# Storing one row block of every eighth tile group in four pieces, so that the 16 DMA engines carry unequal shares

## The chip, the cores and the metric

The kernel runs on one core of a Trainium2 chip. The metric is the device time of one execution in microseconds (us); lower is better. Before the change it is 1296.68 us, the median of three runs (1296.31 to 1297.33).

## What is computed

The input `x` is 8 x 32 images of 512 x 512 in float32. Every group of two channels is normalized (mean and variance over both images), the result goes through three levels of a wavelet pyramid, and `x` is added:

```python
def _wavelet_pyramid(x, levels=3):
    K = outer([.25,.5,.25], [.25,.5,.25])
    result = x
    for level in range(levels):
        sh, sw = (H // 2 ** level, W // 2 ** level)
        approx = conv2d(result[:, :, :sh, :sw], K, padding='SAME')
        result[:, :, :sh // 2, :sw // 2] = approx[:, :, ::2, ::2]
    return result
x = x + _wavelet_pyramid(group_norm(x, G=16))
```

Each level replaces the top left quarter of the region before by its smoothed and halved picture. Everything outside the top left 256 x 256 of an image is only `x + normalized x`. So 268.4 MB are read, 268.4 MB are written, and each element is scaled at least once.

## The kernel before

The 256 images make 128 groups of two channels. A group is one tile of 128 partitions x 4096 float32, 2 MB (16 KB per partition): partition p holds, for each of the two channels and each half of the image, two adjacent image rows. So the tile has four row blocks of 4 KB per partition (channel 0 top half, channel 0 bottom half, channel 1 top half, channel 1 bottom half), and in the DRAM a block of one partition is 4 KB on end. `xs` has eight such tiles, the slots; group n lies in slot n mod 8 and stays there from its load to its store, being changed in place. Sixteen laps of eight groups make the 128 groups.

- **SP** only issues the loads (L149), one DMA of 2 MB per group, in order. From the second lap on each first waits until the store of the group that had the slot before has landed (L148).
- **VectorE** (DVE), once a load has landed, makes horizontal sums of column pairs and of row pairs (L322, L328, L334), then adds the pyramid's results into the tiles of the two groups before (L294, L297, and L309 for the corner of the third level).
- **TensorE** does the vertical part of the three levels as matmuls, and the sums over partitions for mean and variance.
- **ScalarE** (ACT) makes the moments (L452, L457), the square root (L477), moves results out of PSUM (L468, L469, L484) and scales each tile by 1 + r (L491, L496). **GpSimd** (POOL) makes the small coefficients and the pair sums.

In step u of a lap the vector engine begins group u, its level 1 is added one step later (`LAG`), and its corner two steps later (`LAG_L3`). ScalarE also issues the stores: in `step` it calls `store(lap, u - LAG_L3)` right after the moments of group u. `store` (L499) waits on three semaphores and then issues one DMA of 2 MB (L505). The DMA issue stands in ScalarE's own instruction stream, so what follows on that engine (L491 first) isn't dispatched before it. The last two groups are stored in halves of 1 MB by `store_half` (L508, L515) at the end. A DMA adds 16 to its semaphore when it has landed in full.

Each of these DMAs is laid out as 128 partitions x 4 blocks of 4 KB: 512 packets, which over 16 engines are 32 packets and 128 KB for each engine.

Of the kernel before, what the change touches and what calls it, by code (L numbers as in the profile page):

```python
# [10 lines left out]
P = 128  # L11
HP = P // 2
EPS = 1e-5
CG = 2
HALVES = 2
RPP = 2
SLOTS = 8
LAG = 1
LAG_L3 = 2
PAD = 2  # L20
# [2 lines left out]
def pyramid_kernel(nc: bass.Bass, x: bass.AP, out: bass.AP):  # L23
    B, C, H, W = x.shape
# [4 lines left out]
    W1, W2, W3 = W // 2, W // 4, W // 8  # L29
    assert H == HALVES * RPP * P and G % SLOTS == 0 and G > SLOTS and CG * W1 <= 512  # L30

    def groups(a):
        return a.rearrange("b (g c) (f p s) w -> (b g) p (c f) (s w)", c=CG, f=HALVES, s=RPP)

    x_dram = groups(x).rearrange("(l k) p h n -> l k p h n", k=SLOTS)
    out_dram = groups(out).rearrange("(l k) p h n -> l k p h n", k=SLOTS)
    out_half = groups(out).rearrange("(l k) p (c f) n -> l k f p c n", k=SLOTS, f=HALVES)

    with ExitStack() as ctx:  # L40
        def sb(name, shape, dt=F32):
            return ctx.enter_context(nc.sbuf_tensor(name, shape, dt))
# [4 lines left out]
        def sem(name):  # L47
            return ctx.enter_context(nc.semaphore(name))

        xs = sb("xs", [P, SLOTS, ROWS * W])
        h1 = sb("h1", [P, 2, ROWS, W1])
# [36 lines left out]

        x_loaded = [sem(f"x_loaded{i}") for i in range(SLOTS)]  # L90
        x_stored = [sem(f"x_stored{i}") for i in range(SLOTS)]
# [28 lines left out]
        LAPS = G // SLOTS  # L120
# [3 lines left out]
        def exists(base, k):  # L124
            return not isinstance(base, int) or 0 <= base + k < G

        def later(base, k, n):
            return not isinstance(base, int) or base + k >= n

        def rows(slot):  # L130
            return xs[:, slot, :].rearrange("p (r w) -> p r w", w=W)

# [8 lines left out]
        def whole(slot):  # L141
            return xs[:, slot, :].rearrange("p (h n) -> p h n", n=RPP * W)

        @block.sync
        def _(sp):
            def load(lap, slot):
                if later(lap, 0, 1):
                    sp.wait_ge(x_stored[slot], 16 * lap)  # L148
                sp.dma_start(whole(slot), x_dram[lap, slot]).then_inc(x_loaded[slot], 16)  # L149

            for lap in range(LAPS):
                for slot in range(SLOTS):
                    load(lap, slot)

            for slot in range(SLOTS):
                sp.wait_ge(x_stored[slot], 16 * (LAPS + (slot >= SLOTS - LAG_L3)))

        @block.gpsimd
        def _(pool):  # L160
# [83 lines left out]
            def step(lap, u):  # L244
                base = lap * SLOTS
                k = u - LAG
                if exists(base, k):
# [29 lines left out]
        def _(dve):  # L277
# [34 lines left out]
            def step(lap, u):  # L312
                base = lap * SLOTS
                b = u % 2
                k = u - LAG
                make = exists(base, u)
# [35 lines left out]
        def _(pe):  # L352
# [69 lines left out]
            def step(lap, u):  # L422
# [5 lines left out]
                if exists(base, u):  # L428
                    level1(base, u)
                if exists(base, u - LAG):  # L430
                    level2(base, u - LAG)

# [10 lines left out]
        def _(act):  # L443
# [55 lines left out]
            def store(lap, k):  # L499
                n = lap * SLOTS + k  # L500
                slot, back = k % SLOTS, k // SLOTS
                act.wait_ge(scaled, n + 1)
                act.wait_ge(l1_added, n + 1)
                act.wait_ge(l2_added, n + 1)
                nc.scalar.dma_start(out_dram[lap + back, slot], whole(slot)).then_inc(x_stored[slot], 16)  # L505

            def store_half(lap, k, f):  # L508
# [8 lines left out]
            def step(lap, u):  # L517
                base = lap * SLOTS
                make, done = exists(base, u), exists(base, u - LAG)
                if make:  # L520
# [3 lines left out]
                if done:  # L524
                    scale_beside(base, u - LAG)
                if make:
# [32 lines left out]
```

## Time and profile before

| what | value |
|---|---|
| median of three runs | 1296.68 us |
| the profiled execution | 1297.06 us |
| its span, first to last instruction | 1295.1 us |
| DVE / ACT / PE / POOL busy | 93% / 88% / 86% / 58% of the span |
| DMA traffic | 537.03 MB in 135213 packets, mean 415 GB/s |
| granted TensorE clock, mean | 0.991 |

The span and the profiled time differ by 2.0 us, which lie around the instructions. Busy shares are means over the whole run; where a stretch of the run matters, the views were asked for that stretch alone. "DMA share" is the mean busy share of the core's 16 DMA engines; packets overlap a little, so that a full house reads as 1.02 or 1.03. The records name the queue of a packet (q1 holds the loads issued by SP, q10 the stores issued by ACT) but not its engine.

### The profile page before, as it was taken

What the parts mean: (1) busy time and instruction counts of PE and PEld (TensorE: products, weight loads), DVE (VectorE), ACT (ScalarE), POOL (GpSimd) and SP (SyncE); (2) the same over time, 40 slices, a digit from 0 to 9 for tenths busy, and PEclk for the clock granted to TensorE, in tenths of its full rate; (3) what the DMA queues carried; (4) which work ended last, traced back from release to release, by engine and by line L of the source; (5) the groups of instructions that cost most, each with busy time, mean ns of one, the idle gap of its engine ahead of it and who ended that gap; (6) DMA issues with size and microseconds to landing.
All of it is one profiled execution on the core that took longest, in us unless ns stands there. A gap on an engine that the chain in (4) does not pass through costs nothing.

```text
span 1295.1 us, 18208 instructions
## 1 busy us (share of the span) xinstructions
PE 1114.5 (86%) x5120; PEld 608.6 (47%) x5120; DVE 1201.6 (93%) x1536; ACT 1139.1 (88%) x1282; POOL 754.1 (58%) x1445
## 2 busy tenths in 40 slices
PE   5888888888888888888888888888898888888884
PEld 2544444444444444444444444444444444444443
DVE  5899999999999999999999999999899999988994
ACT  4999999999999999999999999999898988879985
POOL 3565665665665666566566566566455654554652
PEclk9999999999999999999999999999999999999998
DMA  9999999999999999999999999999999999999996
GB/s 376 409 419 420 420 421 421 421 421 421 421 422 421 421 421 422 421 421 421 421 421 421 421 421 421 421 421 421 421 421 421 421 421 421 420 414 414 418 407 255
DMA packets 135213, 537.03 MB, mean 415 GB/s; under 512 B 4128, under 2 KB 4128, under 8 KB 135200
## 3 DMA queue, kind: packets, MB, share of 16 engines
q1 hardware_dynamic: 67584, 268.44, 50.7%
q10 hardware_dynamic: 67616, 268.44, 50.5%
q8 instruction: 5, 0.08, 0.0%
q14 instruction: 8, 0.07, 0.0%
HBM read 268.44 MB, written 268.44 MB: 415 GB/s over the span
## 4 chain that ended last, share of the span: by engine, by line
DVE 44%; issue 20%; PE 16%; DMA 13%; ACT 5%; ACTq 1%; DVEq 0%
DVE h L328 16%; DVE xs L297 12%; DMA y_dram<-xs 8%; DVE h L322 7%; DVE xs L294 6%; DMA xs<-x_dram 4%; PE mean_ps L365 3%; PE l_ps L416 3%; PE l_ps L419 2%; PE l_ps L417 2%; PE l_ps L418 2%; ACT squares L457 2%; ACT xs L496 1%; DVE ve L284 1%; DVE r L283 1%
## 5 line engine op out<-in xcount | busy, mean ns | idle before, releaser
L266 POOL TENSOR_TENSOR l_pad<-l_pad,col_fix 128x4 f32<-128x4 f32 x128 | 241.7, 1888 | 484.7 <-ACT l_pad L469 484.7
L457 ACT ACTIVATE squares<-xs,negm 128x4096 bf16<-128x4096 f32 x128 | 474.8, 3709 | 4.2
L322 DVE SCALAR_TENSOR_TENSOR h<-xs 128x2048 f32<-128x2048 f32 x128 | 293.6, 2294 | 14.5 <-DMA xs<-x_dram 10.8
L328 DVE SCALAR_TENSOR_TENSOR h<-xs,h 128x2040 f32<-128x2040 f32 x128 | 291.1, 2274 | 0.0
L496 ACT ACTIVATE xs<-xs,negmr,r_plus 128x2048 f32<-128x2048 f32 x128 | 267.9, 2093 | 0.0
L297 DVE SCALAR_TENSOR_TENSOR xs<-l_pad,r,xs 64x256 f32<-64x256 f32 x256 | 205.2, 841 | 1.8
L491 ACT ACTIVATE xs<-xs,negmr,r_plus 128x1024 f32<-128x1024 f32 x128 | 157.4, 1230 | 27.3 <-issue 27.3
L365 PE MATMUL mean_ps<-hsum,mean_w 128*128 128x1 f32 x256 | 49.1, 261 | 144.3 <-DVE h L328 144.3
L309 DVE SCALAR_TENSOR_TENSOR xs<-l_ps,r,xs 64x256 f32<-64x256 f32 x256 | 123.0, 480 | 46.9 <-PE l_ps L419 45.0
L334 DVE SCALAR_TENSOR_TENSOR a<-h 128x1024 f32<-128x1024 f32 x128 | 158.1, 1235 | 4.4
L223 POOL TENSOR_TENSOR newt<-r,half_t 128x1 f32<-128x1 f32 x128 | 148.5, 1160 | 0.0
L379 PE MATMUL l_ps<-h,w_even 128*64 128x512 f32 x256 | 139.9, 629 | 0.0
L380 PE MATMUL l_ps<-h,w_prev 128*64 128x512 f32 x256 | 139.9, 628 | 0.0
L387 PE MATMUL l_ps<-a,w_odd 128*64 128x512 f32 x256 | 137.2, 618 | 0.0
L468 ACT ACTIVATE l_pad<-l_ps,negm_e 128x512 f32<-128x512 f32 x128 | 88.0, 688 | 55.3 <-PE l_ps L387 55.3
L378 PE MATMUL l_ps<-h,w_prev 128*128 128x512 f32 x256 | 134.8, 609 | 0.0
L241 POOL TENSOR_TENSOR pairs<-l_pad 128x512 f32<-128x512 f32 x128 | 134.5, 1051 | 0.0
L382 PE MATMUL l_ps<-a,w_even 128*64 128x512 f32 x256 | 131.7, 596 | 0.0
L383 PE MATMUL l_ps<-h,w_even 128*64 128x512 f32 x256 | 131.7, 596 | 0.0
L385 PE MATMUL l_ps<-a,w_even 128*64 128x512 f32 x256 | 130.7, 592 | 0.0
L384 PE MATMUL l_ps<-a,w_odd 128*64 128x512 f32 x256 | 130.7, 592 | 0.0
L294 DVE SCALAR_TENSOR_TENSOR xs<-l_pad,r,xs 128x256 f32<-128x256 f32 x256 | 119.7, 504 | 3.7 <-POOL r L230 3.7
(81 smaller groups left out, 1989.1 us busy)
## 6 DMA issues: line engine op xcount, KB each, us to landing
xs<-x_dram SPq DMA_DIRECT2D x128, 2048.0 KB, 15.4
y_dram<-xs ACTq DMA_DIRECT2D x126, 2048.0 KB, 27.9
y_dram<-xs ACTq DMA_DIRECT2D x4, 1024.0 KB, 10.2
```

What stands on the lines that cost most here:

```text
L223: nc.gpsimd.tensor_tensor(newt[:, b, 3:4], r0[:, c], half_t[:], ALU.mult)
L266: nc.gpsimd.tensor_tensor(col, col, col_fix[:, b], ALU.add).then_inc(l1_fixed, 1)
L294: nc.vector.scalar_tensor_tensor(right, l1v[:, :, s, W2:W1], r[:, d], right, ALU.mult, ALU.add)
L297: last = nc.vector.scalar_tensor_tensor(below, l1v[HP:P, :, s, 0:W2], r[HP:P, d], below, ALU.mult, ALU.add)
L322: nc.vector.scalar_tensor_tensor(h1[:, b], v[:, :, 0:W:2], 2.0, v[:, :, 1:W:2], ALU.mult, ALU.add).then_inc(h1_part, 1)
L328: nc.vector.scalar_tensor_tensor(h1[:, b, :, 1:W1], v[:, :, 1:W - 2:2], 1.0, h1[:, b, :, 1:W1], ALU.mult, ALU.add, accum_out=hsum[:, b:b + ...
L334: nc.vector.scalar_tensor_tensor(av, hp[:, :, 0], 2.0, hp[:, :, 1], ALU.mult, ALU.add).then_inc(a1_ready, 1)
L379: nc.tensor.matmul(odd_t, mid, hv[:, 0, :, 1], start=True, stop=False)
L380: nc.tensor.matmul(even_b, prev, hv[:, 1, :, 1], start=False, stop=False)
L457: nc.scalar.activation(squares[:], xs[:, u % SLOTS, :], ACT.Square, bias=negm[:, b:b + 1], accum_out=sumsq[:, b:b + 1]).then_inc(sumsq_rea ...
L491: nc.scalar.activation(beside, beside, ACT.Identity, bias=negmr[:, c], scale=r_plus1[:, c])
L496: nc.scalar.activation(bottom, bottom, ACT.Identity, bias=negmr[:, c], scale=r_plus1[:, c]).then_inc(scaled, 1)
```

## The change

The store of slot 3, so one store in eight (16 of the 128), is issued as four DMAs in place of one. The first takes three of the four row blocks of all partitions (128 x 3 packets of 4 KB, 1.5 MB). The last block (channel 1, bottom half), two image rows per partition, goes in three pieces with packets of 2 KB: its first image row for all 128 partitions, its second image row for the partitions 0 to 118 (119 = 7 x 17), and the second row of the nine partitions left. All four add to the same semaphore, so the waits on slot 3 count 64 per lap where they counted 16. No arithmetic and no other store is changed.

```diff
+SPARED = 3
+        def stores_of(slot):
+            return 4 if slot == SPARED else 1
...
-                    sp.wait_ge(x_stored[slot], 16 * lap)
+                    sp.wait_ge(x_stored[slot], 16 * stores_of(slot) * lap)
...
-                sp.wait_ge(x_stored[slot], 16 * (LAPS + (slot >= SLOTS - LAG_L3)))
+                sp.wait_ge(x_stored[slot], 16 * (stores_of(slot) * LAPS + (slot >= SLOTS - LAG_L3)))
...
-                nc.scalar.dma_start(out_dram[lap + back, slot], whole(slot)).then_inc(x_stored[slot], 16)
+                dst, src = out_dram[lap + back, slot], whole(slot)
+                if slot != SPARED:
+                    nc.scalar.dma_start(dst, src).then_inc(x_stored[slot], 16)
+                    return
+                quarter, most = CG * HALVES - 1, 7 * 17
+                nc.scalar.dma_start(dst[:, 0:quarter], src[:, 0:quarter]).then_inc(x_stored[slot], 16)
+                nc.scalar.dma_start(dst[:, quarter, 0:W], src[:, quarter, 0:W]).then_inc(x_stored[slot], 16)
+                nc.scalar.dma_start(dst[0:most, quarter, W:], src[0:most, quarter, W:]).then_inc(x_stored[slot], 16)
+                nc.scalar.dma_start(dst[most:P, quarter, W:], src[most:P, quarter, W:]).then_inc(x_stored[slot], 16)
```

The change is described as sending one row in eight "over 119 partitions in seven shares and a rest of nine partitions, so that DMA engine 7 has less". Over 16 engines a DMA of 128 partitions gives eight partitions to each; seven shares of 119 partitions are 17 partitions for each of seven engines, and nine partitions are one for each of nine.

## Rows read from the trace of the kernel before

**Rows 1.** The page's first part: busy time, share of the span, instructions.
```profile
PE 1114.5 (86%) x5120; PEld 608.6 (47%) x5120; DVE 1201.6 (93%) x1536; ACT 1139.1 (88%) x1282; POOL 754.1 (58%) x1445
```

**Rows 2.** The page's second and third part: 40 slices of 32.4 us, and queues.
```profile
DMA  9999999999999999999999999999999999999996
GB/s 376 409 419 420 420 421 421 421 421 421 421 422 421 421 421 422 421 421 421 421 421 421 421 421 421 421 421 421 421 421 421 421 421 421 420 414 414 418 407 255
DMA packets 135213, 537.03 MB, mean 415 GB/s; under 512 B 4128, under 2 KB 4128, under 8 KB 135200
...
q1 hardware_dynamic: 67584, 268.44, 50.7%
q10 hardware_dynamic: 67616, 268.44, 50.5%
```

**Rows 3.** Line L322, one per group, from 100 to 870 and 890 to 1270 us.
```profile
L322 DVE SCALAR_TENSOR_TENSOR h<-xs x79: 2292/2293/2298, 107.2 to 869.2; 128x2048 f32<-128x2048 f32 x79
...
L322 DVE SCALAR_TENSOR_TENSOR h<-xs x38: 2291/2293/2327, 888.7 to 1262.8; 128x2048 f32<-128x2048 f32 x38
...
  DMA xs<-x_dram: 2.0, 7
```

**Rows 4.** Stores (L505), ns of an issue, then landing, at 120, 560 and 1100 us.
```profile
L505 ACTq DMA_DIRECT2D y_dram<-xs x8: 383/383/389, 124.4 to 192.8; - x8
...
DMA to landing us min/median/max: 14.6/15.2/15.9
...
L505 ACTq DMA_DIRECT2D y_dram<-xs x8: 383/383/384, 564.0 to 632.4; - x8
...
DMA to landing us min/median/max: 26.3/27.3/28.3
...
L505 ACTq DMA_DIRECT2D y_dram<-xs x10: 383/2346/4347, 1098.9 to 1190.7; - x10
...
DMA to landing us min/median/max: 34.9/36.8/37.6
```

**Rows 5.** Loads (L149), issue and landing, from 400 to 800 and 1000 to 1250 us.
```profile
L149 SPq DMA_DIRECT2D xs<-x_dram x39: 367/368/368, 409.4 to 792.5; - x39
...
DMA to landing us min/median/max: 15.3/15.4/16.2
...
L149 SPq DMA_DIRECT2D xs<-x_dram x25: 367/368/368, 1004.2 to 1246.6; - x25
```

**Rows 6.** Waits of SP's queue, 400 to 800 us: total, times, longest.
```profile
SPq L149 <- DMA y_dram<-xs: 378.1, 39, 10.4
```

**Rows 7.** Stretches at the end; the last two columns are DMA share and GB/s.
```profile
1267.50:1270.50 3.00, 2.88 (x16) 1.76 (x18) 2.73 (x7) 2.64 (x4) 2.77 (x9) 1.00 0.07 26
1282.00:1286.00 4.00, 1.01 (x8) 0.82 (x8) 0.96 (x2) 0.00 (x0) 0.00 (x0) 0.80 1.02 401
...
1290.50:1294.50 4.00, 0.00 (x0) 0.00 (x0) 0.00 (x0) 0.00 (x0) 0.00 (x0) 0.50 0.06 24
```

**Rows 8.** ACT in order of time around one store, steady part: start, us.
```profile
601.15 3.71 ACT L457 ACTIVATE squares<-xs,negm 128x4096 bf16<-128x4096 f32 x1
603.07 0.38 ACTq L505 DMA_DIRECT2D y_dram<-xs  x1
...
604.86 1.23 ACT L491 ACTIVATE xs<-xs,negmr,r_plus 128x1024 f32<-128x1024 f32 x1
```

**Rows 9.** Waits of ACT over the run: total, times, longest.
```profile
ACT xs L491 <- issue: 27.3, 29, 2.5
```

**Rows 10.** ACT in order of time around a store at 1098 us.
```profile
1098.93 2.49 ACTq L505 DMA_DIRECT2D y_dram<-xs  x1
...
1101.47 1.24 ACT L491 ACTIVATE xs<-xs,negmr,r_plus 128x1024 f32<-128x1024 f32 x1 [0.70 <-issue]
```

**Rows 11.** The first eight load issues (L149), which wait for no store.
```profile
L149 SPq DMA_DIRECT2D xs<-x_dram x8: 427/3952/5006, 0.8 to 20.4; - x8
...
DMA to landing us min/median/max: 7.9/22.8/29.0
```

## The prediction

> **What bounds the kernel now.** I read the page's busy shares first: DVE has 93% and ACT 88% [rows 1], which looks like a compute bound. The slices say something else: the DMA engines are full in all slices but the last, at a flat 421 GB/s [rows 2]. So I asked for one line per group. L322 starts every 762.0 / 78 = 9.77 us up to 870 us, and every 374.1 / 37 = 10.11 us from 889 us on, where loads begin to be waited for, if only for 2.0 us in all [rows 3]. Something with a pace of about 10.1 us per group has caught up with a compute pace of 9.77.
>
> The loads show that pace all along: 383.1 / 38 = 10.08 us per issue from 400 to 800 us and 242.4 / 24 = 10.10 later, always 15.4 us to landing [rows 5]. Each load was released by the landing of the store eight groups before [rows 6]. And a store takes ever longer to land: 15.2 us, then 27.3, then 36.8 [rows 4]. Compute eats its lead over the loads, and the lead turns into store backlog.
>
> Whose backlog it is shows at the end. Between 1267.5 and 1270.5 us the DMA share is 0.07 at 26 GB/s, in the last 4 us 0.06 at 24 GB/s, and one engine of 16 is 0.0625 [rows 7]. **One engine works alone** while the others have nothing left. It moves 262144 bytes per group in 10.08 us, 26.0 GB/s. The other 15 move (421 - 26.0) / 15 = 26.33 GB/s each. They aren't idle in the steady part (share 9, flat rate, with always a load queued, since a load takes 15.4 us and the next follows after 10.1); they are only 1.3% quicker. From slice 36 on the rate falls to 414 [rows 2], about what a pace of 10.1 us asks for (4.194 MB / 10.10 us = 415), so there they have run out of backlog.
>
> **The sum, per lap of eight groups.** An engine carries 16 x 128 KiB = 2.097 MB per lap. The slow engine needs 8 x 10.08 = 80.64 us, the others 2.097 / 26.33 = 79.64 us.
>
> Removed from the slow engine, if it is the engine 7 that the change aims at: the plain store gives it eight second-row packets of 2 KB, the new one gives it one of the nine-partition rest. So 14 KiB less, 14336 / 26.0 = 0.55 us: it goes to 80.09 us.
>
> Added to the seven engines with the shares: 17 + 1 in place of 8, so 20 KiB more, 20480 / 26.33 = 0.78 us: 80.42 us. Their packets also grow in number, from 32 to 24 of 4 KB and 26 of 2 KB. A 4 KB packet takes 4096 / 26.33 = 0.156 us. No 2 KB packet is in the trace (all data packets are of 4 KB [rows 2]), so I bound its price by half of that and by all of it. Half gives 80.42 us; all gives 18 packets x 0.156 = 2.81 us more than 79.64, 82.45 us. I take 0.004 us over half, since the engines' rate hardly differs between modes (401 GB/s with stores alone, 421 mixed [rows 2, 7]): 0.1 us, 80.52 us. Three more completion packets lie between nothing and 3 x 0.156 = 0.47 us per lap; the 4128 small packets [rows 2] can't be told apart in the total, and I take nothing.
>
> The Trainium skill (DMA: Bandwidth & Descriptors, "Why small descriptors are slow") gives a fixed 3 cycles per packet beside one cycle per 32 bytes; an estimate from it is 67 / 131 = 51% of a 4 KB packet for a 2 KB one, 0.080 us, and a lap of 80.47 us. The same page ("Why a DMA increments its semaphore by 16 and not by 1") says that 119 partitions go to the lowest seven engines and nine partitions to the lowest nine; no row here names an engine.
>
> So the bound moves from one engine at 80.64 us to seven engines at 80.52 us: 0.12 us per lap, 16 laps, **1.9 us** less. The same over the run: 33.56 MB per engine are 1290.8 us for the slow one and 1274.6 for the others; 16 x 0.88 = 14.1 us more makes 1288.7. The spare time of the others, 16.2 us, is nearly used up by what they are given. The engines past the ninth lose 16 KiB per lap, which bounds nothing.
>
> **ACT** gets three more issues in one group of eight. At 0.38 us each [rows 8] they are 1.15 us. In the steady part the issue ends at 603.45 under the squares, and L491 starts at 604.86, so 1.41 us of cover: no cost. Later an issue takes 2.3 us in the median and up to 4.3 [rows 4], and L491 waits 0.70 us for one that took 2.49 [rows 10], 27.3 us in all [rows 9]. There the additions aren't covered, 16 us at most if each of six late laps adds a full 2.3 + 0.4; but the lead of the loads is gone by then and the engines' backlog goes on draining meanwhile, so I put 0.7 us on the end for it. SP's own additions are nothing: the wait has another constant, and the load it holds is one of a stream that is always 1.5 deep. The tail is the same: the last two groups aren't in slot 3.
>
> The profiled execution had 1297.06 us, the median 1296.68. I forecast 1296.7 - 1.9 + 0.7, rounded up for uneven filling: **1296.0 us**.
>
> **Rivals.**
> - *The seven engines have more room than I think* (24%). Then the slow engine alone still bounds, at 0.55 us less per lap, 8.8 us: 1288 us; in between, the best balance. For it speaks that 421 is a rounded figure, and 26.33 stands only 1.3% over 26.0: an error of 0.1 GB/s in it is 0.3 us per lap, 5 us in the end. Against it: the others' backlog, too, was real, as the flat 421 up to slice 34 is more than the 415 that the kernel asks for in the long run.
 Slot 3's store has 54 packets on the seven engines. It decides from the point where stores need over 30 us to land, some 750 us on: 21 packets more must drain at half an engine's rate, 21 x 0.312 = 6.6 us, less 1.4 of cover, in six laps: 31 us if all of it is on the path, half of it more likely, 1312 us. Against it: the stalls of now already cost compute little beyond the DMA's pace.
> - *The lagging engine is one of the seven* (7%). Then it gets 0.79 + 0.1 us per lap more: 14 us, 1311 us. The trace can't say which it is. The Trainium skill (the same page, "Latency and other measured facts") calls engines 7 and 15 usually slower, but puts it down to descriptor rings that DMAs issued from SP and ACT don't have; by that cause no engine would lag here, and rows 7 show that one does.
> - *A 2 KB packet costs as much as a 4 KB one* (6%): 82.45 - 80.64 = 1.8 us per lap, 29 us, 1326 us. Nothing speaks for it but that no row excludes it.
> - *The shares aren't dealt as described*, and each engine keeps what it had (5%, within "no change"): 1297 us.
>
> **The numbers.** A measurement of this kernel can tell about 0.2%, 2.6 us, from no change. The forecast (46%) and the last rival make 51% for no change; its own range is 1294.1 to 1299.2. Faster is 24%, slower 12 + 7 + 6 = 25%. The range of 1289 to 1308 leaves out the full 8.8 us and the greater part of the slower cases, together under 20%.
>
> **What would show it.** If right: the stores' landing time still climbs to over 30 us, for slot 3 most of all; the loads' pace stays between 10.03 and 10.09 us; the steady rate falls a little below 421 GB/s, as engines past the ninth run dry; and at the end several engines, not one, are last, so that no stretch of 4 us with a share of 0.06 remains. If engine 7 alone still bounds, that stretch stays, the pace is 10.01 us, and the time is 1288. If the pace exceeds 10.2 us, small packets or the wrong engine did it. If L491's waits on issue grow from 27 to over 50 us with the pace unchanged, it was the queue. A time outside 1294 to 1299 makes the forecast wrong.

## The result, and the profile after

The changed kernel takes 1321.91 us, the median of six runs (1320.39 to 1327.71), against 1296.93 us for the kernel before in runs on the same chip (1296.30 to 1297.82): ratio 1.0198, 95% interval 1.0179 to 1.0218. It is 25 us slower. The prediction said 1296.0 us, in a range of 1289 to 1308, and is wrong. The profiled execution took 1320.39 us, its span is 1318.6 us, 23.5 us more than before.

The page of the changed kernel, its busy shares, slices of 33 us and packets:

```profile
PE 1126.9 (85%) x5120; PEld 614.9 (47%) x5120; DVE 1192.2 (90%) x1536; ACT 1138.9 (86%) x1282; POOL 730.1 (55%) x1445
...
DMA  9999999999999999999999999999999999999996
GB/s 375 408 415 420 411 411 421 420 421 420 421 413 409 421 403 419 407 412 421 394 410 421 421 421 374 414 417 412 421 403 421 398 409 421 402 422 403 408 388 261
DMA packets 137774, 537.05 MB, mean 407 GB/s; under 512 B 4640, under 2 KB 4640, under 8 KB 137760
```

Against [rows 1] no compute engine has more instructions; DVE has 9 us less busy time, PE 12 us more. What is new is in the GB/s row: where the kernel before held a flat 421 up to slice 34 [rows 2], now many slices lie at 374 to 413, while the DMA row still shows 9 everywhere. Some engines are full and others are short of work.

The small packets rose from 4128 to 4640, by 512, or 32 per lap. A landing is one small packet per engine (4128 is 16 x 258, and the kernel before has 258 DMAs), and a plain store of 16 landings per lap became 16 + 16 + 7 + 9 = 48. So the count fits shares on seven and on nine engines, though it shows only their sum; the landings further down show the seven. The Trainium skill (DMA: Bandwidth & Descriptors, "Why a DMA increments its semaphore by 16 and not by 1") deals 119 partitions to seven engines and nine to nine; by that rule this count agrees.

Line L327 (L322 before), one per group, in two stretches, 100 to 375 us and 375 to 1295 us:

```profile
L327 DVE SCALAR_TENSOR_TENSOR h<-xs x29: 2291/2293/2303, 97.9 to 371.2; 128x2048 f32<-128x2048 f32 x29
...
L327 DVE SCALAR_TENSOR_TENSOR h<-xs x90: 2291/2294/2316, 381.0 to 1290.6; 128x2048 f32<-128x2048 f32 x90
```

The first stretch runs at 273.3 / 28 = 9.76 us per group, the compute pace of [rows 3]. The second runs at 909.6 / 89 = 10.22 us, and it begins 500 us earlier than the slow stretch of before. The last group starts at 1290.6 us where it started at 1262.8: 27.8 us later, of which 4.3 us come back behind it, in a shorter tail.

The waits of the changed kernel over the whole run (total, times, longest), and SP's queue:

```profile
ACT xs L496 <- issue: 35.7, 13, 6.5
DVE h L327 <- DMA xs<-x_dram: 9.2, 1, 9.2
DVE r L288 <- ACT std L482: 31.1, 16, 5.2
SPq L154 <- DMA y_dram<-xs: 1190.6, 120, 25.0
```

VectorE waits for a load once, for the very first. So the loads are never late, although the DMA engines move less per us than before. The wait that grew is ScalarE's on its own issues: 27.3 us in 29 pieces of 2.5 us at most [rows 9] became 35.7 us in 13 pieces of up to 6.5 us. Few and long is what hurts, since a long one isn't covered. Their place is the issue of the nine-partition piece, L520, here before and after 375 us (min/median/max, ns):

```profile
L520 ACTq DMA_DIRECT2D y_dram<-xs x4: 299/459/782, 67.9 to 302.2; - x4
...
L520 ACTq DMA_DIRECT2D y_dram<-xs x12: 300/3280/4832, 380.2 to 1280.2; - x12
```

One such store in order of time, first on ScalarE, then on VectorE (start, us):

```profile
783.70 3.71 ACT L462 ACTIVATE squares<-xs,negm 128x4096 bf16<-128x4096 f32 x1
785.62 0.38 ACTq L517 DMA_DIRECT2D y_dram<-xs  x1
786.15 0.42 ACTq L518 DMA_DIRECT2D y_dram<-xs  x1
786.73 2.22 ACTq L519 DMA_DIRECT2D y_dram<-xs  x1
789.10 4.83 ACTq L520 DMA_DIRECT2D y_dram<-xs  x1
793.98 1.24 ACT L496 ACTIVATE xs<-xs,negmr,r_plus 128x1024 f32<-128x1024 f32 x1 [6.48 <-issue]
```

```profile
778.18 2.29 DVE L327 SCALAR_TENSOR_TENSOR h<-xs 128x2048 f32<-128x2048 f32 x1
787.94 2.29 DVE L327 SCALAR_TENSOR_TENSOR h<-xs 128x2048 f32<-128x2048 f32 x1
803.64 2.29 DVE L327 SCALAR_TENSOR_TENSOR h<-xs 128x2048 f32<-128x2048 f32 x1
814.48 2.30 DVE L327 SCALAR_TENSOR_TENSOR h<-xs 128x2048 f32<-128x2048 f32 x1
```

The four issues take 7.85 us where one took 0.38. L496 is dispatched 6.48 us late, and the next group on VectorE starts 15.70 us after the one before in place of 9.76. In nine of the twelve laps from 375 us on the last issue is held like this, for 1.15 to 4.83 us. TensorE runs short of work in it, and the clock that it is granted falls (stretch; busy us of PE, PEld, DVE, ACT, POOL; granted clock, DMA share, GB/s):

```profile
780.00:790.00 10.00, 8.84 (x43) 4.91 (x42) 9.67 (x13) 7.13 (x8) 6.04 (x11) 1.00 1.02 420
790.00:800.00 10.00, 3.34 (x17) 3.02 (x16) 3.99 (x6) 5.99 (x9) 3.12 (x6) 0.82 1.03 421
800.00:810.00 10.00, 9.50 (x37) 4.64 (x35) 8.59 (x12) 7.16 (x7) 3.20 (x8) 0.84 0.85 298
```

Means of 0.82 and 0.84 are mixtures of 2.4 and 1.2 GHz. Such stretches are where PE's 12 us come from (mean granted clock of the run 0.981 in place of 0.991); how much of them reaches the time isn't shown.

Landing times tell the same from the other side. The plain stores (L512) land in this, at 120, 560 and 1100 us:

```profile
DMA to landing us min/median/max: 14.9/15.4/16.0
...
DMA to landing us min/median/max: 19.4/22.0/22.8
...
DMA to landing us min/median/max: 22.3/23.7/24.7
```

In the kernel before this climbed to 36.8 us [rows 4]; now it stops at 23.7. The backlog hardly grows any more, as ScalarE is stopped when it tries to put four more DMAs behind it. The DMA engines' delay now reaches compute through the queue of the stores, from 375 us on, and not through late loads.

A stretch of 4 us shortly before the end of the changed kernel, as in [rows 7], with DMA share and GB/s as the last columns:

```profile
1313.00:1317.00 4.00, 0.00 (x0) 0.00 (x0) 0.00 (x0) 0.00 (x0) 0.00 (x0) 0.50 1.01 401
```

No engine works alone in these 4 us.

### The profile page after: what moved, and what is told of

Same layout as the page of the kernel before. It is cut to its first block, busy times and chain, and to the rows that moved or that the text cites. A ratio compares the mean times of both kernels' runs of the same rounds, so it can differ in the third digit from the quotient of the medians.

```text
span 1318.6 us, 18346 instructions
## 1 busy us (share of the span) xinstructions
PE 1126.9 (85%) x5120; PEld 614.9 (47%) x5120; DVE 1192.2 (90%) x1536; ACT 1138.9 (86%) x1282; POOL 730.1 (55%) x1445
## 2 busy tenths in 40 slices
DMA packets 137774, 537.05 MB, mean 407 GB/s; under 512 B 4640, under 2 KB 4640, under 8 KB 137760
## 4 chain that ended last, share of the span: by engine, by line
DVE 46%; PE 21%; issue 21%; ACT 8%; ACTq 3%; DMA 1%; DVEq 0%; POOL 0%; POOLq 0%
DVE h L333 17%; DVE xs L302 12%; DVE h L327 8%; DVE xs L299 7%; PE l_ps L421 4%; PE mean_ps L370 3%; ACT xs L501 2%; PE l_ps L424 2%; PE l_ps L422 2%; PE l_ps L423 2%; PE l_ps L384 2%; PE l_ps L383 2%; PE l_ps L392 2%; ACT squares L462 1%; ACTq L520 1%
## 5 line engine op out<-in xcount | busy, mean ns | idle before, releaser
L271 POOL TENSOR_TENSOR l_pad<-l_pad,col_fix 128x4 f32<-128x4 f32 x128 | 226.4, 1769 | 536.2 <-ACT l_pad L474 536.2
L327 DVE SCALAR_TENSOR_TENSOR h<-xs 128x2048 f32<-128x2048 f32 x128 | 293.8, 2295 | 13.2 <-DMA xs<-x_dram 9.2
L302 DVE SCALAR_TENSOR_TENSOR xs<-l_pad,r,xs 64x256 f32<-64x256 f32 x256 | 192.5, 792 | 1.8
L496 ACT ACTIVATE xs<-xs,negmr,r_plus 128x1024 f32<-128x1024 f32 x128 | 157.3, 1229 | 35.8 <-issue 35.7
L385 PE MATMUL l_ps<-h,w_prev 128*64 128x512 f32 x256 | 142.6, 640 | 0.0
L383 PE MATMUL l_ps<-h,w_prev 128*128 128x512 f32 x256 | 138.6, 624 | 0.0
```

The source lines that it names most:

```text
L271: nc.gpsimd.tensor_tensor(col, col, col_fix[:, b], ALU.add).then_inc(l1_fixed, 1)
L302: last = nc.vector.scalar_tensor_tensor(below, l1v[HP:P, :, s, 0:W2], r[HP:P, d], below, ALU.mult, ALU.add)
L327: nc.vector.scalar_tensor_tensor(h1[:, b], v[:, :, 0:W:2], 2.0, v[:, :, 1:W:2], ALU.mult, ALU.add).then_inc(h1_part, 1)
L383: nc.tensor.matmul(even, w1_prev[:], hv[:, 0, :, 1], start=True, stop=False)
L496: nc.scalar.activation(beside, beside, ACT.Identity, bias=negmr[:, c], scale=r_plus1[:, c])
```

## The experiments

Two causes are to be told apart, called here SEVEN and PIECES. SEVEN: the lagging engine is one of the seven, so that the added load falls on the bound. PIECES: four DMAs in place of one hold ScalarE at its issues, whatever the shares. The expectations, which were written before each run, have letters of their own: A is too many DMAs in ScalarE's queue, B too many packets in it, C uneven shares and small packets that slow the DMA engines themselves; later P stands for the pieces and S for the shares. All runs below are compared with runs of the kernel before on the same chip. Laps and slots are counted from 0.

### The pieces with even shares

`e1_four_even` cuts the store by row blocks, `e2_two_small` into two DMAs with packets of 2 KB only. Both load the 16 engines evenly.

What stands in place of the four issues, in e1 and in e2:

```diff
+                for h in range(CG * HALVES):
+                    nc.scalar.dma_start(dst[:, h:h + 1], src[:, h:h + 1]).then_inc(x_stored[slot], 16)
```

```diff
+                nc.scalar.dma_start(dst[:, :, 0:W], src[:, :, 0:W]).then_inc(x_stored[slot], 16)
+                nc.scalar.dma_start(dst[:, :, W:], src[:, :, W:]).then_inc(x_stored[slot], 16)
```

> Edit: the store of slot 3 is four DMAs, one per row block, all of 128 partitions and 4 KB packets; so four issues, 36 packets per engine in place of 33, even shares. In the changed kernel the fourth issue (L520) takes up to 4.8 us in about every other lap, and the next VectorE groups start 14 to 16 us apart in place of 9.76. Theory A, ScalarE is held because too many DMAs stand in its queue at once: the fourth issue is held here too, by 4 us or more in most laps from 380 us on, and the time is 1312 to 1325 us. Theory B, it is held because too many packets do (54 on the seven engines): 36 is hardly more than 33, nothing is held before 827 us as in the kernel before, and the time is 1296 to 1299. Theory C, the uneven shares and small packets slow the engines themselves: none of either here, 1296 to 1299.

> Edit: the store of slot 3 is two DMAs, each one image row of each of the four row blocks, all of 128 partitions and 2 KB packets; so two issues, 66 packets per engine, even shares. Theory A (number of DMAs): two are at most half as bad as four, held issues short and rare, 1296 to 1303 us. Theory B (number of packets): 66 are more than the 54 of the changed kernel, the second issue is held by 5 us or more in nearly every lap, 1320 to 1335 us. Theory C, if a 2 KB packet costs as much as a 4 KB one: 32 packets x 0.156 = 5 us more per lap on all engines, 80 us, about 1375; at half of it 1297.

Measured: e1 1303.16 us, ratio 1.0052 (1.0035 to 1.0069), +6.3 us; e2 1305.69 us, ratio 1.0068 (1.0052 to 1.0085), +8.8 us. Both lie between the ranges that were expected: the cut alone costs a part of the 25 us, and neither the number of DMAs (A) nor that of packets (B) gives it by itself. And packets of 2 KB are no disaster: e2 has 64 of them per engine and lap in place of 32 of 4 KB, which at full price each would be 32 x 0.156 x 16 = 80 us. But neither has the store of the change, so one more was needed:

`e8_even_halves` keeps the change's first two pieces and halves the other two evenly; `e13_fifteen` makes them 120 and 8 partitions, which 15 and 8 engines take.

```diff
-                quarter, most = CG * HALVES - 1, 7 * 17
+                quarter, most = CG * HALVES - 1, P // 2
```

```diff
-                quarter, most = CG * HALVES - 1, 7 * 17
+                quarter, most = CG * HALVES - 1, 120
```

> Edit against the changed kernel: the last two pieces are partitions 0 to 63 and 64 to 127 in place of 0 to 118 and 119 to 127. Four issues with 24 packets of 4 KB and 16 of 2 KB per engine; every engine carries what it did before the change. The copy without arithmetic took 17.4 us longer with the uneven shares than with even ones. Theory P (the number of pieces holds ScalarE, whatever their shares): 1315 to 1323 us. Theory S (the unequal shares cost 17 us, the pieces the rest): the 6 to 9 us of e1 and e2 remain, 1302 to 1307 us, and ScalarE's held issues cost under 25 us of VectorE's pace.

> Edit against the changed kernel: the last two pieces are 120 partitions (15 x 8) and eight partitions, so that fifteen engines carry eight packets as before, eight of them one more, and the sixteenth eight less. Nearly even shares, but the pieces go to 15 and eight engines, not to all. If the 25 us are the load put on an engine that lags (17 us) and four pieces as such (9 us): 1305 to 1309 us. If a DMA on fewer than 16 engines holds ScalarE by itself: 1313 to 1322 us.

Measured: e8 1305.61 us, ratio 1.0075 (1.0058 to 1.0092), **+8.9 us**; e13 1306.44 us, ratio 1.0076 (1.0059 to 1.0093), +9.6 us. ScalarE's waits on the issue in e8:

```profile
ACT xs L496 <- issue: 27.8, 17, 3.4
```

The last piece's issue over the run, in e8 and then in e13:

```profile
L520 ACTq DMA_DIRECT2D y_dram<-xs x16: 481/882/2442, 67.7 to 1265.8; - x16
```

```profile
L520 ACTq DMA_DIRECT2D y_dram<-xs x16: 283/294/2368, 66.7 to 1266.5; - x16
```

With the same number of DMAs and even shares the last issue takes 0.9 us in the median over the run and 2.4 at most; in the changed kernel, over the run, it takes 1.7 and up to 4.8. Both came out in the range that was expected if the shares cost the rest. So PIECES is real, and worth some 9 us of the 25. A DMA on fewer than 16 engines costs nothing by that alone that these runs could tell: e13 and e8 don't differ beyond their intervals. The uneven shares are the other 16 us (25.0 - 8.9 = 16.1).

The pace per group shows how the two act. L327 in e8, from 100 to 660 us and from 660 to 1280:

```profile
L327 DVE SCALAR_TENSOR_TENSOR h<-xs x57: 2292/2294/3050, 97.9 to 650.0; 128x2048 f32<-128x2048 f32 x57
...
L327 DVE SCALAR_TENSOR_TENSOR h<-xs x62: 2292/2293/3018, 660.1 to 1276.4; 128x2048 f32<-128x2048 f32 x62
```

That is 552.1 / 56 = 9.86 us per group and then 616.3 / 61 = 10.10. The second is the slow pace that the kernel before has from 889 us on (10.11, [rows 3]), only begun some 230 us sooner: the pieces let the slow engine's pace reach compute earlier. The uneven shares change the pace itself, to the 10.22 us of the changed kernel.

### The copy alone: what the uneven shares cost with no compute beside them

`e4_dma_plain` leaves out all arithmetic and keeps the loads and the stores in their order, each store waiting for its load only; its output is a copy of x. `e5_dma_spared` is the same with the change's four pieces in slot 3.

ScalarE's whole program in e4, with the lines that run only in e5 marked (both files hold them; e4 has `SPARED = -1`, e5 `SPARED = 3`):

```diff
             for lap in range(LAPS):
                 for slot in range(SLOTS):
                     act.wait_ge(x_loaded[slot], 16 * (lap + 1))
                     dst, src = out_dram[lap, slot], whole(slot)
+                    if slot != SPARED:
                         nc.scalar.dma_start(dst, src).then_inc(x_stored[slot], 16)
+                        continue
+                    quarter, most = CG * HALVES - 1, 7 * 17
+                    nc.scalar.dma_start(dst[:, 0:quarter], src[:, 0:quarter]).then_inc(x_stored[slot], 16)
...
```

> Leaves out all arithmetic: the same 128 loads by SP into the same eight slots with the same waits, and the same stores of 2 MB by ScalarE, each as soon as its load has landed, so that the output is a copy of the input. It measures the DMA side alone with even shares. If one engine at 26.0 GB/s bounds the kernel before, as the prediction has it, it must carry its 33.56 MB here too: 1285 to 1296 us, and at the end one engine works alone for some us. If the kernel before was bound by compute and its waits after all, the copy is clearly quicker, 1280 us or less.

> The same copy with the four pieces for slot 3, as in the changed kernel; no arithmetic, nothing on ScalarE that an issue could hold up. Theory A or B (only ScalarE's held issues cost): within 4 us of the plain copy, after the prediction's sum 2 us less. Theory C (the shares and the small packets overload the seven engines): 15 to 30 us more than the plain copy. If the lagging engine were one of the seven: 14 us more; if it is one of those spared and the others have room, up to 8.8 us less.

Measured: e4 1280.82 us, ratio 0.9875 (0.9859 to 0.9892); e5 1298.19 us, ratio 1.0008 (0.9998 to 1.0018), so **+17.4 us** for the four uneven pieces, the 15 to 30 us of theory C. e4 itself lies in neither of its two ranges, and no engine works alone at its end: an engine at 26.0 GB/s isn't slow by itself. The page of e4, and its last full stretch (DMA share, GB/s):

```profile
span 1279.1 us, 288 instructions
...
GB/s 368 422 422 421 422 422 421 422 422 421 422 422 421 422 422 421 422 422 421 422 422 421 421 422 421 421 422 421 422 422 421 422 422 421 421 422 421 422 422 404
```

```profile
1270.00:1275.00 5.00, 0.00 (x0) 1.00 1.02 420
```

And of e5, with the two stretches at its end:

```profile
span 1296.3 us, 336 instructions
...
GB/s 371 421 421 422 421 422 421 422 421 421 422 421 421 421 421 422 421 421 422 402 419 414 418 422 404 420 409 418 421 401 417 413 419 421 404 420 409 419 418 323
```

```profile
1285.00:1290.00 5.00, 0.00 (x0) 1.00 0.72 293
1290.00:1296.00 6.00, 0.00 (x0) 1.00 0.38 156
```

In e4 all engines finish together. In e5 a share of 0.38 stands at the end, and seven engines of 16 are 0.44: the seven finish alone, after slices in which the nine ran dry. Here no engine lags before the change, so all of the added load is on the bound: 17.4 / 16 = 1.09 us per lap, where I had 0.88.

The landings say it engine by engine. Each plain DMA leaves one landing record per engine (the updates of its semaphore in the trace), without the engine's name. These are the 16 landings of one store (slot 5), in us after the first of them; "before" is the store of lap 9, e4 lap 9, e5 lap 3, "after" lap 6:

```
before   0.0 0.0 0.2 0.4 0.4 0.6 2.1 2.6 2.7 2.8 2.9 3.0 3.3 3.8 4.5 | 18.0
e4       0.0 0.4 0.5 0.5 0.6 0.6 0.6 0.6 0.7 0.8 0.8 0.8 0.8 1.0 1.1 1.2
e5       0.0 0.0 0.0 0.1 0.1 0.1 0.2 0.4 0.5 | 16.6 16.7 16.7 16.7 16.8 16.8 16.8
after    0.0 0.1 0.1 0.1 0.1 0.1 0.2 0.2 0.3 | 3.0 3.7 5.3 5.7 5.7 6.0 | 13.9
```

Before: one engine lags, and its distance to the 15th landing grows from nothing in lap 2 to 23 us in lap 14. In the copy none does. With the seven loaded in the copy, nine are early and seven late together. In the changed kernel nine are early, **six** late, and one later still; so it is in laps 2 to 6 and 8, and from lap 9 on, with ScalarE held, the six have caught up to within 2.1 us and only the one is late. Had the lagging engine been one of the nine, there would be eight early, seven late and one last.

The store of slot 3 itself tells it once more. Its last six landings in lap 11 of the changed kernel, in us after its first issue:

```
15.1 15.1 | 20.1 22.1 26.3 26.7
```

In each of the laps 9 to 14 four landings stand so behind all others: one engine, once for each piece, 4.2 us between the second and the third (median). An engine outside the seven has no part in the third piece and would have left three at most. And the pace agrees: 8 x 10.22 = 81.8 us per lap is the slow engine's 80.64 with 1.09 on top, 81.7. This is SEVEN, seen; the next runs test it another way.

### Load the seven elsewhere, in other doses

`e10_load_spared` leaves the stores as before and cuts the *load* of slot 3 by the same shares, so that ScalarE has nothing to issue for it. `e11_load_dose` has `CUT = 704`, which moves 5/8 of the bytes.

```diff
+CUT = 512
...
+                sp.dma_start(dst[:, 0:quarter], src[:, 0:quarter]).then_inc(x_loaded[slot], 16)
+                sp.dma_start(dst[:, quarter, 0:CUT], src[:, quarter, 0:CUT]).then_inc(x_loaded[slot], 16)
+                sp.dma_start(dst[0:most, quarter, CUT:], src[0:most, quarter, CUT:]).then_inc(x_loaded[slot], 16)
+                sp.dma_start(dst[most:P, quarter, CUT:], src[most:P, quarter, CUT:]).then_inc(x_loaded[slot], 16)
...
+                    dve.wait_ge(x_loaded[u], (64 if u == SPARED else 16) * (lap + 1))
```

> Edit against the kernel before: the load of slot 3, not its store, is issued in the four uneven pieces; all stores are single DMAs. The engines' shares of bytes are those of the changed kernel, but nothing more stands in ScalarE's queue. If ScalarE's held issues are the greater part of the 25 us: the seven engines' added 17 us against their spare 16 us, 1296 to 1301 us. If the shares alone cost what the change costs: 1310 to 1322 us. L491's waits on issue: at or under 27 us.

> As e10_load_spared, with 5/8 of the dose (the uneven pieces take 320 of the 1024 columns). The seven engines get 5/8 of 17.4, 10.9 us, less than their spare 16; the lagging engine is relieved by 5/8 of 8.8, 5.5 us, if it is among those spared: 1290 to 1293 us. If the lagging engine is one of the seven: 1303 us or more. If the load's pieces cost something of their own: 1295 to 1300 us.

Measured: e10 1325.77 us, ratio 1.0223 (1.0206 to 1.0240), +29.0 us; e11 1319.18 us, ratio 1.0165 (1.0148 to 1.0182), +22.4 us. The waits of e10:

```profile
DVE h L332 <- DMA xs<-x_dram: 36.0, 18, 8.8
...
ACT xs L501 <- issue: 0.2, 1, 0.2
```

ScalarE's waits on its issues are gone and the time is worse. The loads are late now, so the delay comes from the DMA engines and takes whichever way is open. e10 is above both of its ranges; e11 is where it was expected if the lagging engine is one of the seven, 1303 us or more. 3/8 of the dose are 29.0 - 22.4 = 6.6 us, so the whole dose would be 17.6 us. That this is so near e5's 17.4 is in part luck, since the intervals of the two runs leave it open by some 8 us either way. What is left, 11.4 us, would be what doesn't depend on the dose, the four pieces in SP's queue in front of the loads behind them; no run with even pieces of a load shows it by itself. Landings of e10's loads of slots 1 and 5 in lap 6:

```
slot 1   0.0 0.1 0.1 0.1 0.1 0.4 0.7 1.4 2.6 | 11.9 14.4 14.5 14.5 15.1 15.4 | 22.4
slot 5   0.0 0.0 0.1 0.1 0.1 0.3 0.3 0.3 0.6 | 9.2 11.9 11.9 11.9 12.6 13.1 | 22.0
```

Again nine, six and one.

`e9_dose_quarter` keeps the change's stores but sends only the last 128 columns unevenly (packets of 512 B): a quarter of the bytes.

```diff
+CUT = 896
...
+                nc.scalar.dma_start(dst[:, quarter, 0:CUT], src[:, quarter, 0:CUT]).then_inc(x_stored[slot], 16)
+                nc.scalar.dma_start(dst[0:most, quarter, CUT:], src[0:most, quarter, CUT:]).then_inc(x_stored[slot], 16)
+                nc.scalar.dma_start(dst[most:P, quarter, CUT:], src[most:P, quarter, CUT:]).then_inc(x_stored[slot], 16)
```

> Edit against the changed kernel: the uneven pieces take the last 128 columns of a partition's block in place of the last 512, the even piece before them 896, so the seven engines are given 5 KB more per lap in place of 20 and the lagging one 3.5 KB less in place of 14; the pieces, their partitions and their packets stay as many. Theory P, in the form that DMAs on seven or nine engines hold ScalarE: 1315 to 1323 us as with the full dose. Theory S: the seven engines' spare time of 16 us takes a quarter of 17.4 without harm, and 1300 to 1308 us remain.

Measured: 1313.79 us, ratio 1.0134 (1.0117 to 1.0150), +17.0 us. It lies between its two ranges. By the sum it should be 8.9 + 17.4 / 4 = 13.3 us, which is below its interval of 15.2 to 19.4, so the cost doesn't go by the bytes alone.

The landings of slot 3 hold a hint. On the lagging engine the third piece takes, from the landing of the second to its own (median of the laps 9 to 14):

| run | packets of the third piece | it takes | n x (packet + 159 ns) |
|---|---|---|---|
| changed kernel | 17 of 2 KB (84 ns each) | 4.2 us | 4.1 us |
| e9 | 17 of 512 B (27 ns each) | 3.2 us | 3.2 us |
| e13 | 8 of 2 KB | 2.0 us | 1.9 us |
| e8 | 4 of 2 KB | 1.1 us | 1.0 us |

The durations are medians of the packet records in the traces, 159 ns being that of a 4 KB packet. The last column fits if between two packets of the store, of whatever size, the engine moves one 4 KB packet of a load. So a quarter of the bytes still takes three quarters of the third piece's time, and the store queue of that engine is held up by packets and not by bytes. That this is the missing 3.7 us isn't shown by a run.

### Load one engine alone

`e12_first_engine` sends 105 partitions (seven each on 15 engines) and 23 partitions. 23 is no multiple of any number from 2 to 16, so one engine takes them all (its page has 4640 small packets, which is 16 + 16 + 15 + 1 landings per lap for slot 3): with a quarter of the row, 22 KB more per lap for one engine and less for the others.

```diff
+CUT = 768
...
-                quarter, most = CG * HALVES - 1, 7 * 17
+                quarter, most = CG * HALVES - 1, 105
```

> Edit against the changed kernel: the last 256 columns of the block (1 KB packets) go as 105 partitions (15 x 7) and 23 partitions, a prime number that can't be shared out, so all on one engine, the first: it carries 30 KB in these two pieces in place of 8, 22 KB more per lap, the next fourteen carry 1 KB less. If the engine that lags is this first one: its added load goes on the path in full, 16 x 1.1 = 17 us, beside the 9 us that four even pieces cost, 1320 to 1328 us, and in the landings of a late store one engine is far behind 15 that are close together. If it is another of the seven: the first engine's spare 16 us take nearly all of it, 1303 to 1311 us, and two engines land late.

Measured: 1305.21 us, ratio 1.0063 (1.0046 to 1.0080), +8.4 us, which is e8's price for four pieces and nothing on top. 22 KB on the lagging engine would be 22528 / 26.0 = 0.87 us per lap, 14 us. The landings of slot 5 in lap 9, e12 and for comparison e13:

```
e12      0.0 0.1 0.1 0.1 0.2 0.3 0.4 0.6 0.6 0.8 0.8 0.9 0.9 1.0 | 14.4 15.9
e13      (15 landings within 0.6) | 13.2
```

In e12 two engines are late: the one that was loaded, and the one that lags by itself. They aren't the same. (In slot 3's own store seven landings are late, in lap 11 for instance: four of the loaded engine, three of the lagging one, which has no part in the piece of 23.) The spare time of the others, 16 us, took the 14 us in. This is what I had forecast for all seven, and it is the expectation's second case, 1303 to 1311 us. So the lagging engine is in the set of seven and isn't the one that a single share goes to; the Trainium skill (the same section) deals shares from the lowest engine up, and by that it is one of the second to the seventh.

### Ways out that weren't

If the held ScalarE is a loss of its own, other places for the issues should give it back. `e7_rest_later` issues pieces three and four at the end of ScalarE's step. `e3_sp_issues` and `e6_sp_later` have SP issue all four, ahead of the load six or seven groups on.

e7's, behind the last work of the step, and e3's (e6 has `SPARED + 7`):

```diff
+                if exists(base, u - LAG_L3):
+                    store_rest(lap, u - LAG_L3)
```

```diff
+                    if lap > 0 and slot == (SPARED + 6) % SLOTS:
+                        store_spared(lap - 1)
                     load(lap, slot)
```

> Edit against the changed kernel: ScalarE issues the third and fourth piece (119 and nine partitions) at the end of the same step, about 6 us after the first two, behind the scaling and evacuation of that step in place of ahead of them. Same pieces, same shares. Theory A or B: the held time lies where the queue has drained for 6 us, so it shrinks from 33 us in all to under 10, and the time falls to 1293 to 1302 us. Theory C: 1315 to 1322 us as before.

> Edit: the same four pieces for slot 3, issued by SP between its loads (before the load six groups on) in place of ScalarE; packets, shares and bytes as in the changed kernel. Theories A and B: what the change costs is ScalarE held at the issue, so with that gone the time falls back to the DMA engines' pace: 1290 to 1298 us, L496's waits on issue at or under 27 us, VectorE groups 9.76 us apart until the loads are late. Theory C: the engines are slower by the shares themselves and the time stays at 1312 to 1322 us, with waits for loads.

> Edit against e3_sp_issues: SP issues the four pieces one load later, before the load seven groups on. In e3 SP stood 224.3 us in wait for VectorE before it could issue the pieces, with a load due behind them, so loads came late (47.7 us of waits on them). Here that load has gone out before the pieces are ready. Theory A or B: no wait of SP for VectorE over 60 us in total, waits for loads under 10 us, 1291 to 1300 us. If it is the small DMAs that hold whatever queue they are put in, then SP's queue and the loads behind are held in place of ScalarE, and the time stays over 1310 us.

Measured: e7 1316.87 us, ratio 1.0153 (1.0136 to 1.0170); e3 1334.80 us, 1.0282 (1.0260 to 1.0304); e6 1338.90 us, 1.0316 (1.0278 to 1.0354). Waits of e7:

```profile
ACT junk L457 <- issue: 19.5, 6, 5.2
ACT xs L496 <- issue: 18.3, 9, 4.8
```

e7 came out at theory C's 1315 to 1322 us. It saves 5 us of the 25, but the hold only moves to another instruction: 19.5 + 18.3 = 37.8 us against 35.7. Waits of e3 and then of e6:

```profile
DVE h L342 <- DMA xs<-x_dram: 47.7, 25, 8.9
...
SPq L160 <- DVE xs L329: 224.3, 16, 25.3
```

```profile
DVE h L342 <- DMA xs<-x_dram: 51.3, 19, 9.1
```

e6's load issues from 300 to 500 us (min/median/max, ns), and their landing:

```profile
L154 SPq DMA_DIRECT2D xs<-x_dram x19: 367/402/7290, 306.9 to 498.4; - x19
...
DMA to landing us min/median/max: 19.2/29.7/36.2
```

e3 was badly placed: SP waited 224.3 us in all for VectorE's additions, with loads queued behind, so it tells little of the issue itself, and its time is outside both of its ranges. e6 is one load later; SP still waits 78.9 us for VectorE, more than the 60 that were hoped for, and is held by the queue as well, one load issue for 7.3 us, and loads need 29.7 us to land where the changed kernel's need 16.1. Its time stays over 1310 us, as expected if the small DMAs hold whatever queue they are in. Both are worse than ScalarE's queue.

## Why the prediction was wrong, point by point

**What bounds the kernel.** Right, with one thing added. One of 16 engines lags by 1.3%, and the others have spare time: the spans before and of the even copy differ by 1295.1 - 1279.1 = 16.0 us, and I had worked out 16.2. But the engine isn't slow by itself: with no compute beside the DMAs none lags (e4).

**The step that failed: "Removed from the slow engine, if it is the engine 7 that the change aims at".** It isn't one of those that get less. The 14 KiB were taken from an engine that wasn't slow, and the 20 KiB were given to seven engines of which the slow one is a member. The text had this as a rival, "the lagging engine is one of the seven", and gave it 7% and 1311 us. What shows it: nine, six and one landings in the changed kernel and in e10; the four late landings of slot 3's store, one of them in the piece that only the seven carry; e12, where an equal load on another engine costs nothing; and the sizes, since a load that misses the lagging engine has 16.0 us of spare time to go into. I let the change's wording pick the engine though I had written that "the trace can't say which it is". With one engine in 16 unknown and seven given more, 7 / 16 would have been the plain chance, and with the other two slower rivals beside it slower would have been more likely than not. The landing records of the trace before show one engine lagging but don't name it, so only an experiment could.

**"Added to the seven": 0.88 us per lap.** A term mis-sized. It measured 17.4 / 16 = 1.09 us (e5 against e4). The packets aren't to blame for most of the difference: in e5's trace a 4 KB packet takes 159 ns, a 2 KB one 84 and a landing 9 (medians), so that 24 x 159 + 26 x 84 + 3 x 9 - 32 x 159 = 939 ns, or 0.92 us with packets overlapping as a full house of 1.02 says. A 2 KB packet is 4.5 ns over half a 4 KB one, which is the 0.004 us that I took. What the other 0.17 us per lap are isn't shown; a part lies at the end of e5, where the last engines move 156 GB/s in place of the 7 x 26.3 = 184 of seven busy ones. This term alone would have spoiled even the hoped-for case: the copy with these shares takes 1298.19 us, no less than the whole kernel before (ratio 0.9998 to 1.0018), so nothing was left to gain.

**ACT, "0.7 us on the end".** The other mis-sized term, by a factor of ten: four pieces cost 8.9 us with even shares (e8), 9.6 (e13), 6.3 as equal quarters (e1). (In e8, by the durations above, 16 packets of 2 KB and three landings are 0.1 us per lap on every engine, so 1.6 of the 8.9 are the engines' own.) I had looked at the price of one issue [rows 8] and taken the cover for granted early on. But ScalarE was held from 380 us on, when stores landed in some 22 us, not from 750 us. The rival "the queue of the stores fills" (12%, 1312 us) had the right mechanism, the wrong start and about twice the size.

**The sum.** 17.4 + 8.9 = 26.3 us against 25.0 measured (the interval of the ratio is 23.2 to 28.3 us); the 1.6 us of the engines' own in e8 are counted twice in it, without them it is 24.7. e10 and e11 can be written with the same 17.4, as 17.4 + 11.4 and 17.4 x 5/8 + 11.4 = 22.3 (measured 22.4), but the 11.4 was taken from them, and e9 doesn't fit the sum (13.3 against 17.0). So the split is good to some us and not an exact law. Two rivals happened together, priced at 14 and 15 us for parts of some 16 and 9; I had added neither to the other. The range was also narrower than its own chances: it was said to leave out under 20%, while the three slower rivals, 25% together, are all priced above 1308 us.

**"A 2 KB packet costs as much as a 4 KB one"**, 1326 us, lies nearest to the result and is wrong: it would make e5 45 us slower than e4 (2.81 x 16), not 17.4, and e2 some 80 us slower, not 8.8; in the traces a 2 KB packet takes 84 ns beside 159.

**What would show it.** The text said that a pace over 10.2 us means small packets or the wrong engine. The pace is 10.22 us per group, and it was the wrong engine. It said that the stores' landing time would climb to over 30 us, for slot 3 most of all. Plain ones need 23.7 us; the last landing of slot 3's came 25.1 to 30.4 us after its first issue in the laps 4 to 14, over 30 only once. It expected L491's waits on issue (L496 now) at over 50 us for a full queue: 35.7 us were enough, in long pieces. I read the size of the total where the longest mattered.

**Left open.** Which of the six it is, and why an engine lags only when there is compute beside the DMAs. One natural suspect, the fetching of instructions, doesn't fit. The page of the kernel before has (packets, MB, share):

```profile
q8 instruction: 5, 0.08, 0.0%
q14 instruction: 8, 0.07, 0.0%
```

None of these 13 packets lies between 160 and 735 us of the trace, while the engine's distance in slot 5 grows from 1.4 us at 333 to 7.9 at 648. Nor is it one chip's fault: the runs were made on several chips, and one engine of the seven is late alike in e7, e10 and e12, on three of them, while e4 has none on the chip of e7. What exactly holds an issue is open too: e1 has four DMAs and 36 packets per engine with landings, e2 two DMAs and 66, and both are held alike (23.3 and 29.3 us in all), so neither number alone is the rule. No version beat the kernel before. To take work from the lagging engine alone one would need a cut that leaves it out, and each cut tried here gives shares to it, or costs some 6 to 9 us for its pieces, of a gain of at most 16.

## What to carry to other kernels

Before work is moved between DMA engines, find out which engine is behind: a trace that shows one lagging doesn't name it, but loading a known set and counting early and late landings does, and a copy-only version of the kernel gives the spare time of the others in one run. Price the pieces apart from the shares: three more DMA issues cost 9 us here, because the engine that issues them also computes and its queue was backed up long before any load was late. When two rivals don't exclude each other, write down their sum as a case too.

## What the runs showed of the hardware that was not expected

- A plain load-and-store stream of one core runs at 421 to 422 GB/s with all 16 engines level to 1.2 us; with the arithmetic beside it, one engine falls behind by 1.3%, 23 us by lap 14. The same engine's set was late in the loads and in the stores.
- An issue can be held without any load being late: DMA issue on ScalarE took up to 4.83 us, and in the nine laps with a hold it ended 0.4 to 3.0 us after the last landing of the store two before, and the other 15 engines had landed that store 3.4 to 10.7 us before the last one. In the kernel before, held issues ended 3.0 to 4.7 us ahead of the last landing of the store three before. So an issue goes by the most backed-up engine, not by the mean.
- Packet durations are close to a fixed part and a part by size: 9 ns for the 4 bytes of a landing, 27 for 512 B, 46 for 1 KB, 84 for 2 KB and 159 for 4 KB (medians in e9, e12 and the changed kernel).
- With uneven shares the mean DMA traffic falls (407 GB/s in place of 415) while the slices still show 9 tenths busy. The flatness of the GB/s row, not the busy digit, told that engines ran dry.
- Which queue is used matters: the change's four store pieces cost 25 us when ScalarE issues them and 38 and 42 us when SP does (e3, e6).
